# Convolution of tiles 8 to 15 from split operands on unpadded blocks, with moved neighbour parts

## The chip, the cores and the metric

The kernel runs on one core of a Trainium2 chip. Its engines are TensorE (PE; its weight loads are listed as PEld), VectorE (DVE), ScalarE (ACT), GpSimd (POOL) and SyncE (SP), which here only issues DMAs. The engines run side by side and wait for each other by semaphores. The time is that of the device for one launch, in microseconds.

## The reference

Two layers work on x of shape (32, 64, 1024). In a layer a convolution over the last axis (layer 0) or a mixture of eight 1x1 kernels, one set of weights for each sample (layer 1), is followed by a feed-forward product of size 1024 x 1024 with a low-rank part that is chosen for each row by a gate; x is added.

```python
# layer 0
out = lax.conv_general_dilated(x, weight, window_strides=(1,), padding=[(4, 4)],
          dimension_numbers=('NCH', 'OIH', 'NCH'), feature_group_count=4)    # 64 channels, 9 taps, 4 groups
h = out + ctx[:, :, None] + bias[None, :, None]
y = einsum('bsd,od->bso', h, W) + b
sel = the one of x@A[:r].T@B[:, :r].T, r in (8, 16, 32, 64), with the highest score, times its weight
x = x + y + sel
# layer 1: the same shape of work, with einsum('boi,bih->boh', agg_w, x) + agg_b in front,
# and sparsemax weights over 8 experts of rank 16 behind
```

## The kernel before

**Tiles and pairs.** The 32 samples are taken two at a time: a tile is 128 rows (2 samples x 64 channels) of 1024 values; there are 16 tiles. Two tiles are a pair; pairs 0 to 7 are layer 0, pairs 8 to 15 are layer 1. Pairs 0 and 1 are computed plainly while weights are prepared; from pair 2 on (`FULL`) each pair's 256 x 1024 x 1024 product is made from seven products of half size (P1 to P7, Strassen and Winograd's form) of blocks A11, A12, A21, A22 of the mixed input and of their sums S1 to S4 with blocks of the weight and their sums, plus a plain part (`plain`) for the columns that are left.

**Split operands.** The matmuls of the products take a faster form of float32 (fp32r) with fewer bits. So each operand is split: ScalarE casts it to its high part, VectorE subtracts that from the value for the low part (`split_a`, `split_s`, `prep_split`), and TensorE adds three products: high x high, high x low, low x high (`product`, L1379, L1381, L1382).

**The convolution.** The data of a tile is loaded as `blk`: on the partitions 16 channels of a group x 8 positions, in the free dimension 2 samples x 4 groups x 129 blocks of positions (one more than 128, since the rows are padded by 4 on each side). `conv_half(T, n, bank)` (L1328) does one sample: 4 groups x 2 sides, each an unsplit float32 matmul with a block of `blk` stationary and 128 columns of a banded matrix of the taps moving; the second side takes the blocks one further on and adds. VectorE adds the context row and writes the sum to `mixed` (`sum_mix`, L904). TensorE computes the convolution of pair g+1 during pair g, four halves laid between the products, in layer 1 `mix_half` in their place.

**The order of a pair.** It is written out by hand, engine by engine, and each engine follows its list in order. TensorE: plain parts of both tiles, P1, a half, P2, a half, the transpose of the gated rank values (`turn_pair`), P4, P5, a half, the first tile's rank part (`lora`), P6, a half, the second tile's, P7, P3, the rank parts of the second halves. VectorE: gate of the first tile, low parts of S2 and S4, gate of the second, then the sums of the products (`take`), of the plain part (`take_plain`) and of the convolution as they come, the low parts of the next pair's A blocks (L912), of the prepared weights of layer 1 (L861, pairs 3 to 6) and of S1 and S3 (L919). ScalarE: the casts and the gate's exponentials. GpSimd: in pairs 3 to 6 four sums of weight blocks (`prep`, from L529), then the four S sums of the next pair (`sums`, L514 to L522), written in place into `mixed`, after VectorE has made the low parts of the A blocks. SP: loads and stores, in a fixed order.

PSUM has eight banks: b_p0 and b_p1 for the plain parts, b_x, b_y, b_z, b_w for products, b_m and now and then another for the convolution, b_u for transposes.

## Time and profile before

| | us |
|---|---|
| median of 3 runs | 501.63 (501.43 to 501.89) |
| profiled execution | 501.08 |
| its span | 499.3 |
| TensorE busy | 494.9 (99%) |
| VectorE busy | 357.1 (72%) |
| ScalarE busy | 132.5 (27%) |
| GpSimd busy | 141.9 (28%) |

The span runs from the first to the last instruction of the profile; the execution's own time has 1.8 us more around it. Matmuls are pipelined, so that the time that one costs in a stream is read from the start of one to the start of the next (0.20 us for 432 columns), not from its duration (0.36). A line such as L1328 is a line of the kernel; "idle before" says how long the engine stood still ahead of an instruction and what ended that.

### The profile page before, as it was taken

To read this page: it belongs to the slowest core of one execution; us is meant where nothing else is said; L and a number is where in the kernel's file an instruction comes from. 1 tells how busy PE (TensorE), PEld (TensorE's weight loads), DVE (VectorE), ACT (ScalarE), POOL (GpSimd) and SP (SyncE) were. 2 spreads that over 40 slices of the span, in tenths; PEclk is the share of its full clock that TensorE was granted. 3 is DMA by queue.
4 is the path that set the end of the run, shared out by engine and by line. 5 is a ranking of instruction groups with operands and counts; after the bars stand their busy time and mean duration, and the time that the engine had idled before them with its cause. 6 is when DMAs were issued, how large, how long until landed. Compare 5 with 4: busy or idle time off the path is not lost.

```text
span 499.3 us, 8273 instructions
## 1 busy us (share of the span) xinstructions
PE 494.9 (99%) x2921; PEld 459.6 (92%) x2921; DVE 357.1 (72%) x829; ACT 132.5 (27%) x272; POOL 141.9 (28%) x122
## 2 busy tenths in 40 slices
PE   8999999999999999999999999999999999999997
PEld 8989999999999999999999988898998989899886
DVE  4966998758676787767899878676747558675754
ACT  4732344322333123331252321121212112111200
POOL 1000010013444133432205453340616225062520
PEclk9999999999999999999999999999999999999999
DMA  8945205438466475656999553333415232340312
GB/s 319 324 140 175 89 1 159 149 103 267 157 216 220 175 234 189 213 178 224 358 414 347 240 174 101 127 113 130 139 59 173 84 128 105 111 164 1 127 43 84
DMA packets 41124, 84.32 MB, mean 169 GB/s; under 512 B 3803, under 2 KB 16731, under 8 KB 41084
## 3 DMA queue, kind: packets, MB, share of 16 engines
q1 hardware_dynamic: 32028, 61.42, 36.7%
q10 hardware_dynamic: 9056, 22.38, 11.9%
q8 instruction: 23, 0.38, 0.3%
q14 instruction: 17, 0.14, 0.1%
HBM read 58.82 MB, written 24.97 MB: 168 GB/s over the span
## 4 chain that ended last, share of the span: by engine, by line
PE 94%; DMA 2%; DVE 1%; issue 1%; SPq 0%; POOL 0%; ACT 0%; DVEq 0%
PE b_p L1362 9%; PE b_x L1382 7%; PE b_x L1381 7%; PE b_x L1379 7%; PE b_m L1328 5%; PE b_p L1363 4%; PE b_y L1382 4%; PE b_y L1379 4%; PE b_y L1381 4%; PE b_m L1338 3%; PE b_y L1328 3%; PE b_z L1381 2%; PE b_z L1382 2%; PE b_z L1379 2%; PE b_w L1382 2%; PE b_w L1379 2%
## 5 line engine op out<-in xcount | busy, mean ns | idle before, releaser
L596 ACT CAST a_hi<-mixed 128x512 fp32r<-128x512 f32 x63 | 38.1, 620 | 157.5 <-DVE mixed L907 78.6
L1362 PE MATMUL b_p<-wp,a_hi 128*128 128x464 f32 (+1 forms) x224 | 72.6, 377 | 0.0
L542 POOL TENSOR_TENSOR xs<-xs,mixw_sb 128x512 f32<-128x512 f32 x28 | 35.9, 1293 | 121.8 <-DMA xs<-x_scratch 76.0
L919 DVE TENSOR_TENSOR s_lo<-mixed,s_hi 128x512 fp32r<-128x512 f32 x56 | 44.0, 815 | 27.0 <-ACT s_hi L608 27.0
L1363 PE MATMUL b_p<-wp,a_lo 128*128 128x232 f32 (+1 forms) x224 | 60.1, 268 | 0.0
L608 ACT CAST s_hi<-mixed 128x512 fp32r<-128x512 f32 x56 | 34.7, 620 | 86.2 <-POOL mixed L514 50.0
L912 DVE TENSOR_TENSOR a_lo<-mixed,a_hi 128x512 fp32r<-128x512 f32 x63 | 44.3, 731 | 8.8 <-ACT a_hi L596 8.3
L514 POOL TENSOR_TENSOR mixed<-mixed 128x512 f32<-128x512 f32 x13 | 16.7, 1288 | 108.9 <-DVE a_lo L912 108.9
L1362 PEld LDWEIGHTS b_p<-wp,a_hi 128*128 128x128 f32 x224 | 42.1, 188 | 5.1
L1363 PEld LDWEIGHTS b_p<-wp,a_lo 128*128 128x128 f32 x224 | 42.8, 191 | 0.7
L1379 PE MATMUL b_y<-wb_hi,s_hi 128*128 128x464 f32 (+2 forms) x112 | 41.4, 370 | 0.0
L1382 PE MATMUL b_y<-wb_hi,s_lo 128*128 128x464 f32 (+2 forms) x112 | 40.8, 364 | 0.0
L1381 PE MATMUL b_y<-wb_lo,s_hi 128*128 128x464 f32 (+2 forms) x112 | 40.7, 364 | 0.0
L1025 DVE TENSOR_TENSOR xs<-b_x,xs 128x464 f32<-128x464 f32 (+2 forms) x52 | 33.2, 638 | 7.8 <-PE b_x L1382 6.8
L1328 PE MATMUL b_m<-first_in,blk 128*128 128x128 f32 x240 | 29.3, 275 | 0.4 <-DMA blk<-in_xblk 0.4
L1328 PEld LDWEIGHTS b_m<-first_in,blk 128*128 128x128 f32 x240 | 28.9, 192 | 0.7 <-issue 0.5
L1379 PE MATMUL b_x<-wb_hi,s_hi 128*128 128x432 f32 (+1 forms) x80 | 29.3, 367 | 0.0
L1381 PE MATMUL b_x<-wb_lo,s_hi 128*128 128x432 f32 (+1 forms) x80 | 29.2, 365 | 0.0
L1382 PE MATMUL b_x<-wb_hi,s_lo 128*128 128x432 f32 (+1 forms) x80 | 29.1, 364 | 0.0
L1025 DVE TENSOR_TENSOR xs<-b_y,xs 128x512 f32<-128x512 f32 (+2 forms) x26 | 17.0, 654 | 15.8 <-PE b_y L1382 14.2
L1379 PEld LDWEIGHTS b_y<-wb_hi,s_hi 128*128 128x128 f32 x112 | 21.0, 188 | 2.2
L1382 PEld LDWEIGHTS b_y<-wb_hi,s_lo 128*128 128x128 f32 x112 | 21.0, 188 | 1.8
(272 smaller groups left out, 1207.8 us busy)
## 6 DMA issues: line engine op xcount, KB each, us to landing
blk<-x_scratch SPq DMA_DIRECT2D x16, 512.0 KB, 3.9
xs<-in_x SPq DMA_DIRECT2D x30, 256.0 KB, 3.3
x_scratch<-xs SPq DMA_DIRECT2D x30, 256.0 KB, 4.6
blk<-in_xblk SPq DMA_DIRECT2D x14, 516.0 KB, 4.4
xs<-x_scratch SPq DMA_DIRECT2D x28, 256.0 KB, 3.0
out_dram<-xs SPq DMA_DIRECT2D x27, 256.0 KB, 2.1
w_raw<-in_wcat SPq DMA_DIRECT2D x8, 546.0 KB, 8.8
praw<-in_wcat ACTq DMA_DIRECT2D x8, 464.0 KB, 6.1
```

The source lines that it names most:

```text
L542: pool.tensor_tensor(x_rows, x_rows, bbase[:, a:b], ALU.add).then_inc(x_biased[q], 1)
L596: act.copy(a_hi[:, op, :, :], mixed[:, op, :, :]).then_inc(ahi_done[op], 1)
L608: act.copy(s_hi[:, i, :, :], mixed[:, S_AT[i], :, :]).then_inc(shi_done[i], 1)
L912: dve.tensor_tensor(a_lo[:, op, :, :], mixed[:, op, :, :], hi(a_hi[:, op, :, :]), ALU.subtract).then_inc(alo_done[op], 1)
L919: dve.tensor_tensor(s_lo[:, i, :, :], mixed[:, S_AT[i], :, :], hi(s_hi[:, i, :, :]), ALU.subtract).then_inc(slo_done[i], 1)
L1025: dve.tensor_tensor(x_rows, src[:, 0:n], x_rows, ALU.add).then_inc(done, 1)
L1328: ins = pe.matmul(dst, source[:, at + side:at + side + QB], taps, start=(side == 0), stop=(side == 1))
L1362: pe.matmul(both, x_hi, wp[:, k, :, 0:PLAIN[l]], start=(k == 0), stop=False, skip_group_check=True)
L1363: ins = pe.matmul(dst, x_lo, wp_hi[:, k, 0:PLAIN[l]], start=False, stop=(k == NCH - 1), skip_group_check=True)
L1379: pe.matmul(dst, x_hi[:, k, :], w_hi[:, k, :], start=(first and k == 0), stop=False, skip_group_check=not first)
L1381: pe.matmul(dst, x_hi[:, k, :], w_lo[:, k, :], start=False, stop=False, skip_group_check=not first)
L1382: ins = pe.matmul(dst, x_lo[:, k, :], w_hi[:, k, :], start=False, stop=(k == HK - 1), skip_group_check=not first)
```

## The change

For tiles 8 to 15, which are computed during pairs 3 to 6, the convolution takes another form:

- The block is loaded without padding (`xwhole`, 1024 columns). ScalarE casts each sample of it (`cast_x`) and VectorE makes the low part (`low_x`); the taps are split once, at the end of pair 2 (`cast_taps`, `low_taps`).
- A step (`shift_step`) does two groups of one sample: each group three fp32r matmuls with 256 moving columns, for the block of positions itself and, in the same pass, what it gives to its left and right neighbour. Eight steps a pair take the place of four halves.
- VectorE adds the context to the middle 256 columns of the bank (`sum_shift`); ScalarE copies the outer 256 (the neighbours' parts) to SBUF (`take_z`), four DMAs move them by one partition (`move_z`), and GpSimd adds them to `mixed` (`add_z`). The A blocks of those tiles are cast only after that.
- GpSimd's S sums go to a place of their own (`s_sums`) and wait for the products that used them before and no longer for the low parts of A.
- The gates of the two tiles of pairs 2 to 7 are computed together (`gate_scores`, `gate_weights`: the operations of one gate with two tiles side by side, except for two scans and two exponentials).
- In pairs 3 to 6 all engines have a written order of their own (`shift_pair`). In TensorE's P6 now stands ahead of P5. The load of `b_base` moves from pair 3 to pair 7, as its place in SBUF is also used by the cast of x.

The diff, cut to its core; the order of ScalarE and VectorE is shown as rows behind it.

```diff
+def shifted(T):
+    return SHIFTED <= T < TILES
+def steps(T):
+    return 2 * T + 2 * max(0, min(T, TILES) - SHIFTED)
...
+                if shifted(T):
+                    sp.dma_start(blk[T % 2][:, 0:D], xwhole[T - SHIFTED]).then_inc(blk_loaded[T % 2], 16)
...
+            def move_z(T, n):
+                src, dst = z_out[n], z_moved[n]
+                sp.wait_ge(z_taken, 2 * sample(T, n) + 2)
+                if sample(T, n) == 0:
+                    sp.wait_ge(zeroed, 3)
+                if sample(T, n) > 1:
+                    sp.wait_ge(z_added, sample(T, n) - 1)
+                sp.dma_start(dst[1:EDGE + 1, 0, :], src[0:EDGE, 1, :]).then_inc(z_landed[n], 16)
+                sp.dma_start(dst[0:EDGE, 1, :], src[1:EDGE + 1, 0, :]).then_inc(z_landed[n], 16)
+                sp.dma_start(dst[EDGE + 1:P, 0, :], src[EDGE:P - 1, 1, :]).then_inc(z_landed[n], 16)
+                sp.dma_start(dst[EDGE:P - 1, 1, :], src[EDGE + 1:P, 0, :]).then_inc(z_landed[n], 16)
...
             def sums(g):
-                n = 4 * (g - FULL)
-                pool.wait_ge(alo_done[A21], g + 1)
-                pool.wait_ge(alo_done[A22], g + 1)
-                pool.tensor_tensor(mixed[:, A22, :, :], mixed[:, A21, :, :], mixed[:, A22, :, :], ALU.add).then_inc(s_sum, 1)
-                pool.wait_ge(alo_done[A11], g + 1)
+                n, users = 4 * (g - FULL), made(g - 1)
+                pool.wait_ge(p_done[P5], users)
+                if shifted(2 * g):
+                    pool.wait_ge(z_added, sample(2 * g + 2, 0))
+                else:
+                    pool.wait_ge(sum_done, steps(2 * g + 2))
+                pool.tensor_tensor(s_raw(S1), mixed[:, A21, :, :], mixed[:, A22, :, :], ALU.add).then_inc(s_sum, 1)
+                pool.wait_ge(p_done[P7], users)
+                pool.tensor_tensor(s_raw(S3), mixed[:, A11, :, :], mixed[:, A21, :, :], ALU.subtract).then_inc(s_sum, 1)
+                pool.wait_ge(p_done[P6], users)
                 pool.wait_ge(s_sum, n + 1)
-                pool.tensor_tensor(mixed[:, A21, :, :], mixed[:, A11, :, :], mixed[:, A21, :, :], ALU.subtract).then_inc(s_sum, 1)
-                pool.wait_ge(s_sum, n + 2)
-                pool.tensor_tensor(mixed[:, A11, :, :], mixed[:, A22, :, :], mixed[:, A11, :, :], ALU.subtract).then_inc(s_sum, 1)
-                pool.wait_ge(alo_done[A12], g + 1)
+                pool.tensor_tensor(s_raw(S2), s_raw(S1), mixed[:, A11, :, :], ALU.subtract).then_inc(s_sum, 1)
+                pool.wait_ge(p_done[P3], users)
                 pool.wait_ge(s_sum, n + 3)
-                pool.tensor_tensor(mixed[:, A12, :, :], mixed[:, A12, :, :], mixed[:, A11, :, :], ALU.subtract).then_inc(s_sum, 1)
...
+            def add_z(T, n):
+                s = T % 2
+                dst = mixed[:, 2 * s:2 * s + 2, :, CH * n:CH * n + CH].rearrange("p q a c -> p (q a) c")
+                pool.wait_ge(sum_done, steps(T) + 2 * n + 2)
+                pool.wait_ge(z_landed[n], 64 * (T - SHIFTED + 1))
+                pool.tensor_tensor(dst, dst, z_moved[n][:, :, :].rearrange("p v (a c) -> p (v a) c", c=CH),
+                                   ALU.add).then_inc(z_added, 1)
...
+            def cast_x(T, n):
+                act.wait_ge(blk_loaded[T % 2], 16 * (T // 2) + 16)
+                if T == SHIFTED:
+                    act.wait_ge(agg_mm, 3)
+                else:
+                    act.wait_ge(mix_done, steps(T - 1) + 2 * n + 2)
+                act.copy(xh[:, n, :], blk[T % 2][:, BANK * n:BANK * (n + 1)]).then_inc(shift_hi, 1)
+            def take_z(T, n, gp):
+                act.wait_ge(sum_done, steps(T) + 2 * n + gp + 1)
+                if sample(T, n) > 1:
+                    act.wait_ge(z_landed[n], 64 * (T - SHIFTED))
+                src = shift_bank(gp)[:, :].rearrange("p (b a c) -> p b a c", b=4, a=4)[:, 0:4:3, :, :]
+                dst = z_out[n].rearrange("p v (a c) -> p v a c", c=CH)[:, :, :, CH // 2 * gp:CH // 2 * (gp + 1)]
+                act.copy(dst, src).then_inc(z_taken, 1)
...
+            def shift_pair(g):
+                a, b = 2 * g + 2, 2 * g + 3
+                split_s(S2, g)
+                split_s(S4, g)
+                prep_load(g)
+                take_z(a, 0, 0)
+                take_z(a, 0, 1)
+                cast_x(b, 0)
+                gate_exp(2 * g)
+                gate_exp(2 * g + 1)
+                take_z(a, 1, 0)
+                take_z(a, 1, 1)
...
+            def sum_shift(T, n, gp):
+                s, g = T % 2, T // 2
+                dve.wait_ge(s_sum, 4 * (g - 1 - FULL) + (4, 2)[s])
+                for i in (2 * s, 2 * s + 1):
+                    dve.wait_ge(alo_done[i], g)
+                dve.wait_ge(ctx_loaded, 16 * g)
+                dve.wait_ge(mix_done, steps(T) + 2 * n + gp + 1)
+                at = CH * n + CH // 2 * gp
+                row = ctx_row[:, s:s + 1, at:at + CH // 2].to_broadcast([P, POS, CH // 2])
+                dst = mixed[:, 2 * s:2 * s + 2, :, at:at + CH // 2].rearrange("p q a c -> p (q a) c")
+                src = shift_bank(gp)[:, P:P + BANK // 2].rearrange("p (a c) -> p a c", c=CH // 2)
+                dve.tensor_tensor(dst, src, row, ALU.add).then_inc(sum_done, 1)
...
+            def low_x(T, n):
+                part = slice(BANK * n, BANK * (n + 1))
+                dve.wait_ge(shift_hi, 2 + sample(T, n) + 1)
+                dve.tensor_tensor(blk_lo[T % 2][:, part], blk[T % 2][:, part], hi(xh[:, n, :]),
+                                  ALU.subtract).then_inc(shift_lo, 1)
...
+            def gate_scores(g):
+                    dve.tensor_reduce(hid_sb[:, HID0 * s:HID0 * (s + 1)],
+                                      wide(s)[:, :, REST[0]:PLAIN[0]].rearrange("p v c -> p c v"), AX_X,
+                                      ALU.add).then_inc(hid_done, 1)
+                dve.wait_ge(hid_done, 2 * (g - FULL) + 2)
+                hid = by_tile(hid_sb[:, 0:2 * HID0])
...
+            def gate_weights(g):
+                dve.wait_ge(exp_done, 2 * g + 2)
+                link(dve.reciprocal(st[:, 4:6], st[:, 2:4]))
+                link(dve.reciprocal(st[:, 6:8], st[:, 4:6]))
+                link(dve.tensor_tensor(st[:, 0:2], st[:, 4:6], st[:, 6:8], ALU.mult))
+                link(dve.tensor_tensor(kept, below, st[:, 0:2].unsqueeze(2).to_broadcast([P, 2, 4]), ALU.mult))
...
+            def shift_step(T, n, gp):
+                pe.wait_ge(shift_lo, 2 + sample(T, n) + 1)
+                for gl in range(2):
+                    at = QB * (2 * gp + gl)
+                    x_hi, x_lo = xh[:, n, at:at + QB], blk_lo[T % 2][:, BANK * n + at:BANK * n + at + QB]
+                    dst = shift_bank(gp)[:, :].rearrange("p (a c) -> p a c", c=2 * GC)[:, :, GC * gl:GC * (gl + 1)]
+                    w_hi, w_lo = (part[:, gp, 2 * P * gl:2 * P * (gl + 1)].rearrange("p (a c) -> p a c", c=GC)
+                                  for part in (taps_hi, taps_lo))
+                    pe.matmul(dst, x_hi, w_hi, start=True, stop=False)
+                    pe.matmul(dst, x_hi, w_lo, start=False, stop=False)
+                    ins = pe.matmul(dst, x_lo, w_hi, start=False, stop=True)
+                ins.then_inc(mix_done, 1)
+            def emptied(T, n, gp):
+                pe.wait_ge(z_taken, 2 * sample(T, n) + gp + 1)
             def mix_half(T, b, dst_bank):
...
+            def shift_pair(g):
+                t1, t2, a, b = 2 * g, 2 * g + 1, 2 * g + 2, 2 * g + 3
+                if g == AGG_PAIR + 1:
+                    pe.wait_ge(agg_read, 4)
+                pe.wait_ge(sum_done, steps(t2 + 1))
+                if shifted(t2):
+                    emptied(t2, 1, 1)
+                shift_step(a, 0, 0)
+                pe.wait_ge(fin12, g)
+                shift_step(a, 0, 1)
+                pe.wait_ge(fin22, g)
+                product_a(g, P1, b_x, A11, B11)
+                emptied(a, 0, 0)
+                shift_step(a, 1, 0)
+                emptied(a, 0, 1)
+                shift_step(a, 1, 1)
+                pe.wait_ge(fin11, g)
+                product_a(g, P2, b_z, A12, B21)
+                emptied(a, 1, 0)
+                shift_step(b, 0, 0)
+                emptied(a, 1, 1)
+                shift_step(b, 0, 1)
+                turn_pair(g)
+                pe.wait_ge(took_w, made(g - 1))
+                product_a(g, P4, b_w, A22, T4)
+                emptied(b, 0, 0)
+                shift_step(b, 1, 0)
+                emptied(b, 0, 1)
+                shift_step(b, 1, 1)
+                lora(t1, b_z, 0, BANK, c11_done)
+                pe.wait_ge(took_p1, made(g))
+                product_s(g, P6, b_x, S2, T2, first=False)
+                emptied(b, 1, 1)
+                product_s(g, P5, b_y, S1, T1)
+                lora(t2, b_w, 0, BANK, c21_done)
+                pe.wait_ge(took_u2, made(g))
+                product_s(g, P7, b_x, S3, T3, first=False)
+                pe.wait_ge(took_p5, made(g))
+                product_s(g, P3, b_y, S4, B22, first=False)
+                pe.wait_ge(fin21, g + 1)
+                lora(t2, b_x, BANK, D, c22_done)
+                lora(t1, b_y, BANK, D, c12_done)
```

VectorE in pair 4 before, from the second tile's last gate product to the low parts of the prepared weights (`mixed<-b_m,ctx_row` is the convolution's sum, 128x8x64 being 512 columns; `ut_hi` is the transposed rank part; `xs0<-b_x` the sum of P1):

```order
L977 TENSOR_SCALAR u_sb<-hid_sb,kw 128x16
L977 TENSOR_SCALAR u_sb<-hid_sb,kw 128x32
L1025 TENSOR_TENSOR xs0<-b_x,xs0 128x432
L904 TENSOR_TENSOR mixed<-b_m,ctx_row 128x8x64
L904 TENSOR_TENSOR mixed<-b_y,ctx_row 128x8x64
L912 TENSOR_TENSOR a_lo<-mixed,a_hi 128x512 x2
L929 TENSOR_TENSOR ut_hi<-b_u,ut_hi 64x128 x2
L861 TENSOR_TENSOR prep_lo<-praw,prep_hi 128x464 x4
```

VectorE in a pair after, from the same place to P6's sum:

```order
L1257 TENSOR_TENSOR u_sb<-hid_sb,kw 128x2x32
L1135 TENSOR_TENSOR blk_lo<-blk,xh 128x512
L1301 TENSOR_TENSOR xs<-b_x,xs 128x432
L1122 TENSOR_TENSOR mixed<-b_m,ctx_row 128x8x32
L1122 TENSOR_TENSOR mixed<-b_y,ctx_row 128x8x32
L1158 TENSOR_TENSOR ut_hi<-b_u,ut_hi 64x128 x2
L1135 TENSOR_TENSOR blk_lo<-blk,xh 128x512
L1122 TENSOR_TENSOR mixed<-b_m,ctx_row 128x8x32
L1122 TENSOR_TENSOR mixed<-b_y,ctx_row 128x8x32
L1060 TENSOR_TENSOR prep_lo<-praw,prep_hi 128x464 x4
L1301 TENSOR_TENSOR xs<-b_x,xs 128x432
L1140 TENSOR_TENSOR a_lo<-mixed,a_hi 128x512 x2
```

The sums are twice as many and half as wide, two low parts of blocks (`blk_lo`) stand between them, the low parts of A have moved behind P6's sum, and that sum, which P7 waits for, stands behind the low parts of the prepared weights; before, P5's sum did.

ScalarE in a pair after, from the z copies of the second tile's first sample (`a_hi_place<-b_m`, in the space of a_hi's A21) to those of its second:

```order
L849 COPY a_hi_place<-b_m 128x8x32
L849 COPY a_hi_place<-b_y 128x8x32
L777 CAST prep_hi<-praw 128x464 x2
L742 CAST ut_hi<-b_u 64x128
L743 CAST ut_lo<-b_u 64x128
L742 CAST ut_hi<-b_u 64x128
L743 CAST ut_lo<-b_u 64x128
L840 CAST xh<-blk 128x512
L849 COPY a_lo_place<-b_m 128x8x32
L849 COPY a_lo_place<-b_y 128x8x32
```

Before, the casts of A11 and A12 stood around the prep casts in that place; now the block's cast and the z copies do.

GpSimd in a pair after, `mixed<-mixed,z_moved` being the addition of the neighbours' parts, which is new:

```order
L632 TENSOR_TENSOR praw<-praw 128x464
L633 TENSOR_TENSOR praw<-praw 128x464
L635 TENSOR_TENSOR praw<-praw 128x464
L637 TENSOR_TENSOR praw<-praw 128x464
L645 TENSOR_TENSOR mixed<-mixed,z_moved 128x8x64 x4
L617 TENSOR_TENSOR s_sums<-mixed 128x512
L619 TENSOR_TENSOR s_sums<-mixed 128x512
L622 TENSOR_TENSOR s_sums<-s_sums,mixed 128x512
L625 TENSOR_TENSOR s_sums<-mixed,s_sums 128x512
```

Four instructions of 512 columns are put between the prep sums and the S sums, which keep their order.

## Rows read from the trace of the kernel before

**Rows 1.** The page's busy times: us, share of the span, instructions.
```profile
PE 494.9 (99%) x2921; PEld 459.6 (92%) x2921; DVE 357.1 (72%) x829; ACT 132.5 (27%) x272; POOL 141.9 (28%) x122
```
**Rows 2.** TensorE's longest wait: for whom, us in total, times, longest.
```profile
PE b_y L1431 <- POOL ones L489: 1.1, 1, 1.1
```
**Rows 3.** Pairs 4 and 7: length; PE, PEld, DVE, ACT, POOL; clock, DMA share, GB/s.
```profile
144.30:175.04 30.74, 30.74 (x190) 29.36 (x189) 22.72 (x57) 8.31 (x20) 10.92 (x9) 1.00 0.56 186
...
236.50:267.00 30.50, 30.50 (x179) 28.88 (x178) 27.25 (x64) 11.88 (x23) 6.86 (x6) 1.00 1.00 379
```
**Rows 4.** Timeline of TensorE, pair 5: start, duration, line, what.
```profile
182.50 1.95 PE L1328 MATMUL b_m<-first_in,blk 128*128 128x128 f32 x16
184.20 0.44 PE L1379 MATMUL b_z<-wb_hi,a_hi 128*128 128x432 f32 x1
184.48 0.36 PE L1381 MATMUL b_z<-wb_lo,a_hi 128*128 128x432 f32 x1
184.68 0.35 PE L1382 MATMUL b_z<-wb_hi,a_lo 128*128 128x432 f32 x1
```
**Rows 5.** Timeline of TensorE, the last product's twelve matmuls, and the next.
```profile
492.44 0.28 PE L1379 MATMUL b_y<-wb_hi,s_hi 128*128 128x256 f32 x1
...
493.85 0.39 PE L1420 MATMUL b_y<-lb,ut_hi 128*128 128x512 f32 x1
```
**Rows 6.** Timeline of VectorE, pair 4: the second gate (first and last row), sums.
```profile
151.58 0.30 DVE L947 TENSOR_REDUCE hid_sb<-b_p 128x68 f32<-128x136 f32 x1
...
154.40 0.60 DVE L1025 TENSOR_TENSOR xs<-b_x,xs 128x432 f32<-128x432 f32 x1
154.92 0.68 DVE L904 TENSOR_TENSOR mixed<-b_m,ctx_row 128x512 f32<-128x512 f32 x1
...
166.83 0.68 DVE L904 TENSOR_TENSOR mixed<-b_m,ctx_row 128x512 f32<-128x512 f32 x1
167.43 0.60 DVE L1025 TENSOR_TENSOR xs<-b_x,xs 128x432 f32<-128x432 f32 x1
```
**Rows 7.** Timelines of VectorE and of GpSimd, pair 7.
```profile
257.38 2.15 DVE L865 TENSOR_TENSOR wb_lo<-wb_raw,wb_hi 128x928 fp32r<-128x928 f32 x2
...
264.61 3.25 DVE L865 TENSOR_TENSOR wb_lo<-wb_raw,wb_hi 128x928 fp32r<-128x928 f32 x2
...
264.87 2.01 POOL L517 TENSOR_TENSOR mixed<-mixed 128x512 f32<-128x512 f32 x1
266.96 2.05 POOL L519 TENSOR_TENSOR mixed<-mixed 128x512 f32<-128x512 f32 x1
```
**Rows 8.** Timelines of VectorE and of GpSimd, around the end of pair 4.
```profile
174.53 1.29 DVE L919 TENSOR_TENSOR s_lo<-mixed,s_hi 128x512 fp32r<-128x512 f32 x1 [1.60 <-ACT s_hi L608]
175.74 0.68 DVE L1025 TENSOR_TENSOR xs<-b_x,xs 128x512 f32<-128x512 f32 x1
...
173.99 1.29 POOL L517 TENSOR_TENSOR mixed<-mixed 128x512 f32<-128x512 f32 x1
175.35 1.62 POOL L519 TENSOR_TENSOR mixed<-mixed 128x512 f32<-128x512 f32 x1
```
**Rows 9.** Groups of ScalarE: shapes, count, busy us, mean ns, idle before.
```profile
L608 ACT CAST s_hi<-mixed 128x512 fp32r<-128x512 f32 x56 | 34.7, 620 | 86.2 <-POOL mixed L514 50.0 <-POOL mixed L519 14.5 <-POOL mixed L517 11.3
L664 ACT COPY kernels_sb<-b_m 64x512 f32<-64x512 f32 x4 | 2.3, 577 | 0.1
```
**Rows 10.** Pair 4: SP's stores and the loads behind them.
```profile
148.81 0.91 SPq L363 DMA_DIRECT2D x_scratch<-xs  x2
156.45 0.81 SPq L358 DMA_DIRECT2D xs<-in_x  x2
```
**Rows 11.** DMA issues: count, KB each, median us to landing.
```profile
x_scratch<-xs SPq DMA_DIRECT2D x30, 256.0 KB, 4.6
...
praw<-in_wcat ACTq DMA_DIRECT2D x8, 464.0 KB, 6.1
...
aggb_scratch<-aggb_sb SPq DMA_DIRECT2D x1, 8.0 KB, 1.3
```

392 lines of the change are left out of this document (310 added, 82 removed).

## The prediction

> **What bounds the kernel now.** First the busy table and the list of waits: TensorE is busy 494.9 us, 99% of the span [rows 1], and its longest wait, for a constant at the start, is 1.1 us [rows 2]. Then a table of stretches, cut at the starts of layer 0's pairs. I count pairs from 0, and those with converted convolutions are 3 to 6, since pair g convolves for pair g+1. Pair 4 takes 30.74 us and TensorE is busy in all of it, at the full granted clock, with VectorE busy 22.7 us and GpSimd 10.9 us [rows 3]; cut in the same way, pairs 3, 5 and 6 are 30.70, 30.74 and 30.72 us long. So a microsecond taken from TensorE there is a microsecond of the kernel, as long as VectorE, ScalarE, GpSimd and the transfers keep ahead. That cover is what I price.
>
> **TensorE's own work.** A convolution half is sixteen recorded matmuls from 182.50 to 184.20, 1.70 us. The first product behind it takes 0.28 us to the next one instead of 0.20, 0.08 more [rows 4]. Four halves a pair: 4 x 1.78 = 7.12 us. The new form has eight steps a pair, each of 2 groups x 3 matmuls of 256 columns. Such matmuls stand in the last product: twelve from 492.44 to 493.85, 0.118 us each [rows 5]. A step is 6 x 0.118 = 0.71 us, eight are 5.6 us. The transpose, which stood behind a convolution half, now stands between split products; I charge the 0.08 us again. Gain: 7.12 - 5.64 - 0.08 = 1.4 us a pair, 5.6 us in four pairs. The profiled execution took 501.08 us, so without any new wait it would take 495.5.
>
> The Trainium skill (TensorE: Matmul & The Clock Gate, Back-to-back issue gap) gives N/2.4 + 2.5 ns for a warm matmul, 109 ns for 256 columns. The row has 118 ns, so I keep the row. By the page the gain would be 0.4 us a pair larger.
>
> **VectorE's work.** Sums: eight of 256 columns for four of 512. A 512-column one takes 0.60 us to its successor, a 432-column one 0.52 [rows 6]; from that 0.34 for 256, so 2.7 against 2.4 us. Low parts of the blocks: four of 512 x 0.60 = 2.4 us. The gates: one takes 2.82 us (151.58 to 154.40) [rows 6], two 5.6; a joint one has two reduces, one more scan and one set of links, which I put at 1.55 for the scores and 1.4 for the weights, 3.0. Net 0.3 + 2.4 - 2.6 = 0.1 us. By the sum of its work VectorE would have 22.8 of 29.3 us to do, and all would be covered.
>
> **The shared reads.** But look at 264.61: two instructions of VectorE that each read two operands in SBUF take 3.25 us where the same two took 2.15 at 257.38, with GpSimd idle, and in that time GpSimd's two last 2.01 and 2.05 us [rows 7] instead of 1.29 [rows 8]. They run strictly in turn: VectorE waits for GpSimd's end, GpSimd for VectorE's. Instructions that read PSUM are not held: a product's sum at 175.74 keeps its 0.68 us beside a GpSimd instruction. The s_lo ahead of it, held until GpSimd's end at 175.28, takes 1.29 us [rows 8]. In a pair of before GpSimd has 8 such instructions, VectorE 12 large ones. After: 12 (four added z parts) and 16 (four low parts). In turn they fill 12 x 1.26 + 16 x 0.60 = 24.7 us of a pair. What counts is which fall together, so I follow one pair, us from its start, with these durations, 0.22 us from the end of a matmul group to VectorE, and ScalarE's 0.62 for 512 columns and an estimated 0.35 for a z copy of 256 from PSUM, below the 0.58 of one with 512 [rows 9].
>
> TensorE without waits, a product being twelve matmuls of 0.196: plain parts to 5.1; steps of the first new tile a to 5.8 and 6.5; P1 to 8.9; steps to 10.3; P2 to 12.7; steps of tile b to 14.1; transpose and P4 to 16.6; steps to 18.0; rank part; P6 from 18.5 to 20.9; P5 to 23.2; rank part; P7 23.7 to 26.1; P3 to 28.4; rank parts to 29.4.
>
> VectorE comes in late from the pair before (s_lo of S1 and S3 now follow the last sums): it starts S2's and S4's at about 5.9, ends at 7.1; sums of a, 7.8; ScalarE's z copy and cast, then the low part, 9.5; scores 11.0; sums 11.7; weights 13.1 (the transpose wants them at 14.1: covered, by 1 us); low part 13.7; P1's sum 14.2; sums of b 14.9. Here it waits: its rank split stands behind ScalarE's prep casts, these behind GpSimd's prep sums, which wait for the gates; GpSimd starts at 13.7, its second ends at 16.0, ScalarE is through at 17.1 and 17.6, VectorE at 18.0. Low part 19.1 (held by a prep sum, 0.3); sums of b 19.8. GpSimd adds the first z from 19.1 to 20.4, then the second: four prep_lo take until 24.0 instead of 22.1. P6's sum 24.5: **P7 starts at 24.6 instead of 23.7**. a_lo held by the third z, to 26.4; two sums 27.6: **P3 waits for P5's, to 27.7 instead of 27.0**. Plain part, P4's sum 28.9; low part 29.5 to 30.8, as GpSimd is then at the last z or S1's sum or not; P7's sum 30.0 to 31.3, for which the last rank parts wait. The pair ends at 31.1 to 32.4; VectorE goes into the next some 5.9 us late, so this repeats.
>
> The ends: 29.4 a pair if no held read and no wait reaches TensorE; 32.4 if every late term falls together. I take 31.4 for pairs 4 and 5, the lower part of my chain, since a held read can also fall where VectorE would wait anyway. Pair 3 starts less late (four tap and block low parts are added ahead of it, but S4's sum comes 2 us earlier since the sums no longer wait for a_lo): 30.9. Pair 6 has no low parts for a next pair: 30.7. Sum 124.4 us against 122.9 before: +1.5.
>
> **The transfers.** Each moved z is four issues at 0.45 us (two took 0.91 [rows 10]) and lands between 1.3 us (8 KB) and 4.6 us (256 KB) later [rows 11]; 16 issues a pair stand in SP's queue. What queues behind them: the x loads, which wait for stores anyway (issued at 148.81, next loads at 156.45 [rows 10]), and the block loads. A block that lands near 18 instead of 15 holds ScalarE's cast and with it sums of b, but VectorE meets the held prep_lo afterwards in any case; 0 to +0.5 a pair, I take 0. The b_base load moves from pair 3 to pair 7, where the transfer engines are full (1.00 busy against 0.56 [rows 3]); GpSimd needs it only in pair 8: 0 to +1.5 us in all, taken 0. Pair 7 itself has VectorE busy 27.25 of 30.5 [rows 3]; it starts later but its gates are 2.6 us shorter: between 0 and +1.5, taken 0. A gain from layer 1 or these is excluded, since TensorE is full there already. The prep transfer, issued at about 5, takes a median of 6.1 us [rows 11] and is there before the gates. The zeroing of two z buffers and the s_sums that are apart from mixed lie beside TensorE's full time: nothing.
>
> Own time: 501.08 + 1.5 = 502.6 us. The median of the runs shown is 0.55 above the profiled execution; the forecast of the median is **503.1 us**.
>
> **The rivals.**
> A. The cover holds. GpSimd's and VectorE's reads meet less than I lay out, or the joint gate is quicker, so that P7 and P3 start on time; pairs of 29.4 to 30.2 us, 117.6 to 120.8 in all: 496.3 to 499.5. For it: on paper VectorE has 6 us a pair to spare, and 1.3 us less of held reads brings my chain to 29.9. Against it: 24.7 us of reads in turn in 29.4. With the 0.4 us a pair of the page's rule the low end would be 494.7.
> B. The waits just eat the gain: pairs of 30.4 to 31.0, 500.6 to 502.6, within 0.2% of before, which is about what a measurement of this kernel can tell from no change. It is my chain with one held read less in each pair.
> C. Slower by the z chain, one mechanism: the last z part of a pair (TensorE at 18.0, VectorE 19.8, ScalarE 20.2, SP from there behind a 512 KB block load, landing 26 to 27) delays GpSimd's last add, all four S sums and the casts of A21, A22 by that much. Its place is the second plain part, which needs a_lo of A21 2.6 us into the next pair, and A22 at 3.8. In my chain A21 is ready at +2.3 and A22 at +4.1 of a pair of 31.4 in the late variant. So it decides as soon as the landing is later than about 27; each us beyond is a us of the pair. Price 1 to 2 us a pair on top: 505.5 to 509.
> D. That the change doesn't do what it says (six matmuls of 0.118 us a step): output written in runs of 16 floats could slow them; the old form wrote such runs too. 3%.
>
> **Chances.** Forecast (pairs around 31.3, 501.5 to 505.5) 0.40; A 0.33; B beside it 0.11; C 0.13; D 0.03. Faster: A and a little of B and of the forecast's low end, 0.37. Within 0.2%: most of B and the low end of the forecast, 0.17. Slower: the rest, 0.46. For eight in ten the range takes in nearly all of A and the lower half of C: 496.3 to 507.0; the likeliest's own range is 500.8 to 505.5.
>
> **What would show it.** A step of six matmuls in 0.71 us, no more 0.08 behind it. VectorE busy over 26 us a pair, s_lo, a_lo, prep_lo and blk_lo with means well above 0.68 us, GpSimd's instructions above 1.3. TensorE's waits naming P6's and P5's sums on VectorE (took_u2, took_p5), some 1 and 0.7 us a pair. Wrong, if the pairs last 29.4 to 30 us with no such waits (A), if TensorE waits for a_lo at the plain part (C), or if it waits for z copies in ScalarE or for the transpose instead, which I have covered by 1 us only.

## The result and the profile after

| | before | after |
|---|---|---|
| median, us | 501.78 (501.43 to 503.69) | 518.49 (517.11 to 521.45) |
| ratio | | 1.034, 95% interval 1.032 to 1.036 |
| profiled execution | 501.08 | 518.63 |
| its span | 499.3 | 516.8 |

The forecast was 503.1 us, the range 496.3 to 507.0: the sign of the likeliest case was right, the size was not. The page's first line, and from its fourth part the shares of the chain that ended last; they answer to [rows 1]:

```profile
PE 497.5 (96%) x2857; PEld 456.8 (88%) x2857; DVE 364.4 (71%) x797; ACT 152.4 (29%) x322; POOL 167.9 (32%) x140
...
PE 62%; DVE 9%; POOL 9%; DMA 7%; issue 7%; SPq 5%; ACT 1%; DVEq 0%; POOLq 0%
```

TensorE makes up 62% of that chain; VectorE, GpSimd, transfers and SP's issues are in it. What TensorE waited for (us in total, times, longest), answering to [rows 2]:

```profile
PE b_p L1725 <- DVE a_lo L1140: 8.4, 4, 2.4
PE b_y L1742 <- ACT a_lo_place L849: 2.0, 3, 1.1
PE b_y L1742 <- DVE xs L1301: 1.9, 4, 0.6
PE b_z L1701 <- DVE xs L1301: 1.7, 1, 1.7
```

The longest is the second plain part's wait for the low part of A21, once each in pairs 4 to 7. The stretches cut at the starts of pairs 3 to 7 and 0.6 us behind the end of pair 7, columns as in [rows 3], and in the last row 4.3 us behind pair 4's wait:

```profile
114.14:144.37 30.23, 29.74 (x175) 27.66 (x174) 23.69 (x55) 11.63 (x31) 9.94 (x8) 1.00 0.75 238
144.37:178.97 34.60, 31.53 (x175) 29.04 (x174) 25.20 (x53) 13.11 (x32) 17.48 (x12) 0.95 0.61 206
178.97:213.98 35.01, 31.57 (x174) 29.15 (x173) 26.00 (x53) 13.15 (x32) 17.54 (x12) 0.95 0.64 208
213.98:248.46 34.48, 30.58 (x174) 27.61 (x173) 24.73 (x51) 11.91 (x30) 16.70 (x12) 1.00 0.63 200
248.46:281.50 33.04, 28.95 (x162) 26.18 (x161) 25.20 (x51) 14.24 (x26) 11.33 (x8) 1.00 0.97 351
149.20:153.50 4.30, 4.30 (x18) 3.92 (x19) 4.26 (x5) 1.24 (x2) 4.16 (x3) 0.60 0.57 206
```

Pair 3 takes 30.23 us, less than its 30.74 before; pairs 4, 5 and 6 take 34.6, 35.0 and 34.5 against 30.74 each, 11.9 us more. From pair 7's start to the end it is 268.3 us against 262.8, 5.5 more, nearly all of it in pair 7: 32.5 us (248.46 to 280.94) against 27.2 (236.52 to 263.68; the stretch of 30.50 us in [rows 3] runs 3.3 us into pair 8). Pair 3 starts 0.6 later and gives 0.5 back. Together that is the 17.5 us of the span. The later start is there before pair 0: TensorE's first split product begins at 11.4 us instead of 10.7, and anywhere from 10.9 to 12.8 in the kernels of the experiments.

TensorE's own gain is there. The timeline of TensorE where pair 3's first steps begin: twelve matmuls from 119.25 to 120.68, 0.71 and 0.73 us a step.

```profile
119.25 0.28 PE L1686 MATMUL b_m<-taps_hi,xh 128*128 128x256 f32 x1
119.95 0.28 PE L1686 MATMUL b_y<-taps_hi,xh 128*128 128x256 f32 x1
120.68 0.35 PE L1742 MATMUL b_x<-wb_hi,a_hi 128*128 128x432 f32 x1
```

**Where pair 3 goes wrong.** SP's issues of the last two z parts of pair 3 and of the block between them, ScalarE's issue of the store of the prepared weights (0.93 MB twice), and GpSimd's last add:

```profile
135.22 0.82 SPq L433 DMA_DIRECT2D z_moved<-a_hi_place  x1
136.09 0.55 SPq L386 DMA_DIRECT2D blk<-in_xwhole  x1
136.75 0.58 SPq L430 DMA_DIRECT2D z_moved<-a_lo_place  x1
137.37 0.60 SPq L431 DMA_DIRECT2D z_moved<-a_lo_place  x1
138.01 0.85 SPq L432 DMA_DIRECT2D z_moved<-a_lo_place  x1
138.90 1.92 SPq L433 DMA_DIRECT2D z_moved<-a_lo_place  x1
...
137.30 0.39 ACTq L785 DMA_DIRECT2D ts_hi_scratch<-prep_hi  x1
137.72 0.59 ACTq L785 DMA_DIRECT2D ts_lo_scratch<-prep_lo  x1
...
145.71 1.29 POOL L645 TENSOR_TENSOR mixed<-mixed,z_moved 128x512 f32<-128x512 f32 x1 [7.07 <-DMA z_moved<-a_lo_place]
```

The moves of 112 rows are out before or with the store, those of 15 rows behind it. The z part has landed at 145.6, 31.4 us into the pair, where the forecast had 26 to 27.

**The loop.** Pair 4 from its casts of A21 and A22 to those of the next pair, ScalarE, VectorE, GpSimd and SP:

```profile
147.03 1.14 ACT L722 CAST a_hi<-mixed 128x512 fp32r<-128x512 f32 x2 [9.72 <-POOL mixed L645]
...
160.64 0.50 DVE L1257 TENSOR_TENSOR u_sb<-hid_sb,kw 128x16 f32<-128x16 f32 x4
...
161.28 1.52 POOL L632 TENSOR_TENSOR praw<-praw 128x464 f32<-128x464 f32 x1 [7.58 <-DVE u_sb L1257]
166.44 2.99 POOL L645 TENSOR_TENSOR mixed<-mixed,z_moved 128x512 f32<-128x512 f32 x2
180.72 1.27 POOL L645 TENSOR_TENSOR mixed<-mixed,z_moved 128x512 f32<-128x512 f32 x1 [6.87 <-DMA z_moved<-a_lo_place]
...
167.80 0.55 SPq L430 DMA_DIRECT2D z_moved<-a_hi_place  x1
174.05 1.67 SPq L433 DMA_DIRECT2D z_moved<-a_lo_place  x1
...
182.03 1.14 ACT L722 CAST a_hi<-mixed 128x512 fp32r<-128x512 f32 x2 [10.03 <-POOL mixed L645]
```

Low parts, sums, the S low parts and the gates until 161.3 (14.3 us), four prep sums to 166.5 (5.2), the first add to 167.8 (1.3), for which SP's move of the third part waits, nine issues to 175.7 (7.9), landing at 180.7 (5.0), the last add (1.3): 35.0 us, about the length of the pair. Each cast of A21 waits for the chain that the one before it started. TensorE is not in this loop; it waits for it.

### The profile page after: what moved, and what is told of

It is laid out like the page before. It is cut to its first block, busy times and chain, and to the rows that moved or that the text cites. A ratio compares the mean times of both kernels' runs of the same rounds, so it can differ in the third digit from the quotient of the medians.

```text
span 516.8 us, 8425 instructions
## 1 busy us (share of the span) xinstructions
PE 497.5 (96%) x2857; PEld 456.8 (88%) x2857; DVE 364.4 (71%) x797; ACT 152.4 (29%) x322; POOL 167.9 (32%) x140
## 3 DMA queue, kind: packets, MB, share of 16 engines
q10 hardware_dynamic: 9056, 22.38, 11.4%
## 4 chain that ended last, share of the span: by engine, by line
PE 62%; DVE 9%; POOL 9%; DMA 7%; issue 7%; SPq 5%; ACT 1%; DVEq 0%; POOLq 0%
PE b_p L1725 5%; DMA z_moved<-a_lo_place 5%; PE b_x L1745 4%; PE b_x L1744 4%; PE b_x L1742 4%; PE b_m L1673 3%; PE b_p L1726 3%; PE b_y L1745 3%; PE b_y L1742 3%; PE b_y L1744 3%; DMA wp_place<-in_wcat 2%; POOL mixed L645 2%; PE b_m L1701 2%; SPq L432 2%; DVE a_lo L1140 2%
## 5 line engine op out<-in xcount | busy, mean ns | idle before, releaser
L1725 PE MATMUL b_p<-wp,a_hi 128*128 128x464 f32 (+1 forms) x224 | 76.5, 391 | 8.6 <-DVE a_lo L1140 8.4
L654 POOL TENSOR_TENSOR xs<-xs,mixw_sb 128x512 f32<-128x512 f32 x28 | 38.6, 1390 | 122.9 <-DMA xs<-x_scratch 87.8
L1140 DVE TENSOR_TENSOR a_lo<-mixed,a_hi 128x512 fp32r<-128x512 f32 x63 | 54.5, 898 | 20.5 <-ACT a_hi L722 20.0
L733 ACT CAST s_hi<-s_sums 128x512 fp32r<-128x512 f32 x56 | 34.7, 621 | 72.5 <-POOL s_sums L617 34.6
L1148 DVE TENSOR_TENSOR s_lo<-s_sums,s_hi 128x512 fp32r<-128x512 f32 x56 | 46.5, 881 | 7.6 <-POOL s_sums L622 7.4
L1726 PEld LDWEIGHTS b_p<-wp,a_lo 128*128 128x128 f32 x224 | 44.4, 198 | 0.6
L645 POOL TENSOR_TENSOR mixed<-mixed,z_moved 128x512 f32<-128x512 f32 x16 | 22.5, 1411 | 38.1 <-DMA z_moved<-a_lo_place 28.7
L617 POOL TENSOR_TENSOR s_sums<-mixed 128x512 f32<-128x512 f32 x13 | 16.6, 1279 | 56.1 <-DVE mixed L1104 35.2
L1301 DVE TENSOR_TENSOR xs<-b_y,xs 128x512 f32<-128x512 f32 (+2 forms) x26 | 17.1, 656 | 15.8 <-PE b_y L1745 14.3
L659 POOL MEMSET kernels_sb<- 128x2048 f32 x1 | 1.8, 1820 | 66.6 <-DVE wb_lo L1034 66.6
L625 POOL TENSOR_TENSOR s_sums<-mixed,s_sums 128x512 f32<-128x512 f32 x13 | 22.6, 1741 | 1.9
```

Source lines behind the costliest of these rows:

```text
L645: pool.tensor_tensor(dst, dst, z_moved[n][:, :, :].rearrange("p v (a c) -> p (v a) c", c=CH), ALU.add).then_inc(z_added, 1)
L654: pool.tensor_tensor(x_rows, x_rows, bbase[:, a:b], ALU.add).then_inc(x_biased[q], 1)
L733: act.copy(s_hi[:, i, :, :], s_raw(i)).then_inc(shi_done[i], 1)
L1140: dve.tensor_tensor(a_lo[:, op, :, :], mixed[:, op, :, :], hi(a_hi[:, op, :, :]), ALU.subtract).then_inc(alo_done[op], 1)
L1148: dve.tensor_tensor(s_lo[:, i, :, :], s_raw(i), hi(s_hi[:, i, :, :]), ALU.subtract).then_inc(slo_done[i], 1)
L1301: dve.tensor_tensor(x_rows, src[:, 0:n], x_rows, ALU.add).then_inc(done, 1)
```

## The experiments

All start from the changed kernel unless another is named. "Before" ran beside each, between 501.35 and 501.86 us. In brackets behind a time stand its ratio to the kernel before and the 95% interval of that ratio.

**Without the moves.** The four DMAs of `move_z` and the two waits for them go (and one wait for `finq` is added ahead of pair 7's loads); GpSimd adds zeros, and the neighbours' parts are missing from the output.

```diff
-                sp.dma_start(dst[1:EDGE + 1, 0, :], src[0:EDGE, 1, :]).then_inc(z_landed[n], 16)
...
-                pool.wait_ge(z_landed[n], 64 * (T - SHIFTED + 1))
```

> Leaves out the moves: no z DMA is issued, GpSimd adds buffers of zeros, so the neighbours' parts are missing from the output. Theory Z (the last z part of a pair lands too late and holds GpSimd's add, the casts of A21 and A22 and so the second plain part): the plain part's waits (8.4 us in pairs 4 to 7) and the slow clock behind two of them (about 3.4 us) go, and with them most of pair 7's extra: 502 to 505 us. Rival V (VectorE and GpSimd are late by themselves, through their reads in turn, as my forecast had it; the landing is only the last to be seen): the plain part still waits over 1.5 us a pair, 512 to 517 us.

512.83 us (1.024, 1.019 to 1.028): the time is in V's range, but its sign, the plain part's wait, isn't there. Another wait stands in its place: P7 waits 1.7 us in pairs 3 to 5 and 1.2 in pair 6 for P6's sum, with the clock low behind the first and the third of these. GpSimd's adds and VectorE's prep low parts in pair 4, and then the window behind pair 3's wait:

```profile
164.94 6.77 POOL L641 TENSOR_TENSOR mixed<-mixed,z_moved 128x512 f32<-128x512 f32 x4
...
166.33 5.88 DVE L1054 TENSOR_TENSOR prep_lo<-praw,prep_hi 128x464 fp32r<-128x464 f32 x4
```

```profile
140.00:144.00 4.00, 4.00 (x12) 3.70 (x13) 3.96 (x8) 1.66 (x3) 0.56 (x1) 0.57 0.92 336
```

Freed from the transfer, four adds run back to back just where VectorE makes four low parts, and these take 5.88 us instead of 2.59 (at 168.99 in the changed kernel). So both theories were partly right: without Z there is V, the forecast's own.

**A later store.** ScalarE issues `prep_store` behind the casts of S1 and S3, and `prep_load` behind the first z copies.

```diff
-                prep_store(g)
                 split_a(A21, g + 1)
                 split_a(A22, g + 1)
                 split_s(S1, g + 1)
                 split_s(S3, g + 1)
+                prep_store(g)
```

> ScalarE issues the store of the prepared weights (1.86 MB) behind the casts of S1 and S3 instead of ahead of those of A21 and A22, and loads the next raw weights behind the first z copies. Theory Z with the transfer as its main part: the last z lands 3 to 5 us earlier, the plain part's waits and the slow clock go, 503 to 508 us. If instead the late issue counts (SP gets to the last z only at 171.4 us, since GpSimd's prep sums hold the z before it): the landing moves by 1 us, 514 to 517 us. Rival V: no change, 518.

521.07 us (1.037, 1.033 to 1.041), slower than all that was expected, but not for V's reason: the waits for A21 are gone. Pair 4's last moves, issued until 174.55, are added from 175.96; in the changed kernel it was 175.72 and 180.72. From the end of the last issue to the add it is 1.4 us against 5.0: the store had made the difference. What ate it is a new wait of TensorE's, in this kernel's list:

```profile
PE b_m L1686 <- ACT a_lo_place L849: 9.3, 3, 3.6
PE b_u L1770 <- issue: 4.1, 1, 4.1
```

`prep_load` waits for the late store in ScalarE's queue, and the second z copies stand behind it.

**The first add ahead of the prep sums.** GpSimd's `add_z(a, 0)` stands before `prep(g)`; ScalarE's `split_ut` before its first two prep casts.

```diff
+                if shifted(2 * g + 2):
+                    add_z(2 * g + 2, 0)
                 if PREP_FIRST <= g <= PREP_LAST:
                     prep(g)
```

> GpSimd adds the first z part ahead of the four prep sums, ScalarE makes the rank split ahead of the prep casts. Theory Z with the late issue as its main part: SP can move the third z 3 us earlier (it waits for the first add), the last one 2 to 3 us earlier, so the plain part's wait falls to under 0.5 us and the clock stays up: 506 to 511 us. With the transfer as main part: the z still lands together with the prep store, 515 to 518. Rival V: 518, or more, as the prep sums end 2 us later.

505.18 us (1.0067, 1.0046 to 1.0089), 13 us less than the changed kernel and a little better than Z said. Pairs 4 and 5, and the waits:

```profile
144.08:174.80 30.72, 29.95 (x174) 27.61 (x173) 24.71 (x54) 13.11 (x33) 17.01 (x13) 1.00 0.74 235
174.80:205.13 30.33, 29.70 (x174) 27.62 (x173) 24.30 (x54) 13.14 (x33) 17.89 (x13) 1.00 0.73 238
```

```profile
PE b_x L1744 <- DVE xs L1303: 2.5, 4, 0.7
PE b_z L1703 <- DVE xs L1303: 2.1, 1, 2.1
```

The loop of 35 us is gone, and what waits now is P7, for P6's sum, as the forecast had it: 0.5 to 0.7 us in the list, 0.8 from one matmul's start to the next (168.90 less 167.88, where 0.23 is usual, in pair 4).

**ScalarE's order alone**, to part the two edits of that kernel:

> The change with ScalarE's new order alone (rank split ahead of the first two prep casts), GpSimd's order left as it was. It parts the two edits of the kernel that took 505 us. If GpSimd's place for the first add is the cause of the gain: 517 to 519 us. If it was ScalarE's order: 505 to 510.

520.76 us (1.039, 1.037 to 1.042): pairs of 35.0, 36.0 and 33.5 us. ScalarE's order gives nothing by itself, so the gain needs GpSimd's place for the first add; whether that place is enough alone was not run.

**The last z ahead of the block load**, in SP's order:

```diff
-                    load_blocks(b + 2)
                     move_z(b, 1)
+                    load_blocks(b + 2)
```

> SP issues the moves of the last z part ahead of the block load of 512 KB. Theory Z: it gains the load's issue (0.6 us) and 512 KB less ahead of it in the queue (about 1.3 us at 400 GB/s): 1 to 2 us a pair in three pairs, and the clock with it in one or both of two: 510 to 515 us. Rival V: no change, 518.

517.29 us (1.030, 1.028 to 1.033), 1.2 less than the 518.49 of the changed kernel, of another comparison, so no more than a hint. Less than Z said: pair 4's last moves went out from 170.8 instead of 171.4, still with the store.

**TensorE kept busy in the wait.** Eighteen matmuls on the constant ahead of the second plain part's first wait, pairs 4 to 7:

```diff
+                    if k == 0 and s == 1 and FULL + 2 <= g < PAIRS:
+                        for _ in range(18):
+                            pe.matmul(both[:, 0, 0:P], ones[:, :], ones[:, :], start=True, stop=True)
```

> The change with 18 matmuls of 128 columns on the constant (about 1.9 us) ahead of the second plain part's wait in pairs 4 to 7, into a bank that the plain part starts anew. If the idle time itself brings the clock down (0.60 granted behind the waits of pairs 4 and 5): it stays at 1.00, 3 to 3.5 us less: 515 us. If the clock follows something else: 518.5, or 519 where the filling overruns the wait.

520.96 us (1.037, 1.034 to 1.040), although the clock stayed up. Its windows over pair 4's start, and over pairs 4 and 5:

```profile
149.00:153.50 4.50, 4.50 (x38) 4.39 (x38) 4.45 (x5) 2.09 (x4) 4.36 (x4) 1.00 0.44 142
145.39:179.60 34.21, 33.58 (x211) 31.82 (x209) 24.05 (x53) 13.15 (x32) 16.96 (x12) 1.00 0.63 202
179.60:215.29 35.69, 33.95 (x210) 31.62 (x209) 24.83 (x53) 13.12 (x32) 16.87 (x12) 1.00 0.64 211
```

With the waits filled the clock stayed up in pairs 4 and 5, where it had been low behind waits of 2.0 and 2.4 us. That idling alone decides it isn't shown: in the kernel with b_base late (below) a wait of 2.2 us in pair 4 left it at 1.00. Either way the 3.5 us that I had charged to the clock were not in the sum: the pairs keep their 34 to 36 us with TensorE at full clock, since the loop sets them.

**One converted pair** (`SHIFTED = 14`; pairs 3 to 5 keep the old convolution):

> Only tiles 14 and 15 take the new form, in pair 6; pairs 3 to 5 keep the old convolution, with the joint gates, the separate S sums and the late load of b_base. If these parts cost nothing by themselves: pairs 3 to 5 as before at 30.7 us, pair 6 30.2, pair 7 with its wait for A21 (1.9) and its other extra (2 to 3): 504.5 to 506.5 us. If they cost 0.5 us a pair (rival): 506.5 to 508.

505.84 us (1.0075, 1.0058 to 1.0092), in the expected range, but by two misses that cancel: pair 6 took 0.9 us less than expected, the wait for A21 1.6 us more. Pairs 3 to 5 take 30.74 us each, so the joint gates and the separate S sums cost nothing. Pair 6, and pair 7's first 31 us, then its wait:

```profile
206.68:235.96 29.28, 29.28 (x174) 27.88 (x173) 22.53 (x53) 10.79 (x29) 11.03 (x8) 1.00 0.68 211
235.96:267.00 31.04, 27.54 (x151) 25.66 (x150) 23.08 (x49) 12.96 (x25) 9.07 (x7) 0.95 0.93 339
```

```profile
PE b_p L1725 <- DVE a_lo L1140: 3.5, 1, 3.5
```

A converted pair without any wait takes 29.28 us: 1.46 less than before. The wait for the last z, 3.5 us, comes after a single such pair; the loop isn't needed for it, but repeats it.

**P6's sum earlier**, behind two of the four prep low parts, on the kernel with the first add early:

> The change with the first add ahead of the prep sums, and besides VectorE takes P6's sum between the second and the third low part of the prepared weights, so that P7 need not wait for all four. If P7's wait of 0.8 us a pair is this queue position: it falls to under 0.2 us, four pairs, 505.2 - 2.5 to 3.3 = 502 to 502.7 us. If VectorE is simply short of time there (reads in turn), the wait moves to P3 or to the low parts of A and 505 us stays.

507.03 us (1.010, 1.008 to 1.013), slower than both. P7's wait is gone; P3 waits instead (0.6, 0.6 and 0.8 us in pairs 3, 4 and 6), P5 once 1.2 us for a z copy and the mixture 2.8.

**b_base loaded last**, on the changed kernel and on the one with the first add early:

```diff
-                if turns:
-                    sp.wait_ge(mix_done, steps(TILES))
-                    sp.dma_start(bbase, b_base.partition_broadcast(P)).then_inc(s_bbase, 16)
...
                 store_x(2, g)
+                if turns:
+                    sp.dma_start(bbase, b_base.partition_broadcast(P)).then_inc(s_bbase, 16)
```

> The change with the load of b_base (512 KB) issued at the end of SP's list for pair 7 instead of at its start. If this load delays the plain weights (ScalarE's cast, VectorE's low part ahead of P2's sum, 1.8 us in which the mixture waits, and 0.6 behind it): 516 to 517 us. If the delay comes from the late second plain part, behind which that load is issued: 518 to 518.5 us.

> The first add ahead of the prep sums and b_base loaded last, nothing else. In that kernel with the early load the plain weights landed 12.3 us after their issue (8.8 before) and the mixture waited 2.1 us, behind it 1.3 us of slow clock. If the b_base load is the cause: 501.5 to 503 us. If it is the other transfers and VectorE's late start: 505.

518.49 us on the first: the mixture's wait of 1.7 us went, the one for A21 in pair 7 grew to 2.8, nothing was gained. On the second 501.49 us (1.0008, 0.9992 to 1.0024): from 1.0067 to 1.0008 of before, 3.0 us. Its profiled execution is a long one, 503.38 us; pairs 4 and 5, with P7's 0.8 us still in each:

```profile
144.52:174.97 30.45, 29.81 (x175) 27.61 (x174) 24.62 (x55) 13.13 (x33) 17.05 (x13) 1.00 0.74 240
174.97:205.53 30.56, 29.93 (x174) 27.61 (x173) 23.86 (x54) 13.09 (x33) 17.08 (x13) 1.00 0.72 233
```

**VectorE's order**, on that kernel: first the sums of P6 and P5 early, then P7's too.

> The first add ahead of the prep sums, VectorE's sum of P6 behind two of the four prep low parts, its sum of P5 behind one low part of A, b_base loaded last. The products' waits (0.8 us a pair for P7, 0.6 for P3 once P6 is early) and the mixture's 2.1 us of pair 7 should all go: from 505.2 less 4 x 0.8 and less 2 to 3.5 (the clock behind it too): 499 to 500.5 us, faster than before. If VectorE is short in the sum, the waits come back at another instruction: 503 to 505.

506.75 us (1.010, 1.008 to 1.013): no product waits, but the last rank part does, 1.7, 1.8 and 1.7 us in pairs 3 to 5, for P7's sum. So P7's sum goes ahead of the first plain sum and of the block's low part:

```diff
+                take(b_x, 2, g, fin21)
                 dve.wait_ge(fin11, g + 1)
                 take_plain(0, g)
                 if shifted(a + 2):
                     low_x(a + 2, 1)
...
-                take(b_x, 2, g, fin21)
```

> As the kernel with the sums of P6 and P5 early and b_base late (506.8 us, where the last rank part waits 1.8 us a pair for P7's sum), but VectorE takes P7's sum ahead of the first plain sum and of the low part of the block. If VectorE only has its work in the wrong order: no product and no rank part waits, pairs of 29.4 to 30 us, 498 to 500.5 us, faster than before. If VectorE is short of time in the second half of a pair (its reads held by GpSimd's): the wait comes back at a fourth place, A21 or the sums of the convolution, 501.5 to 506.

501.31 us (1.0001, 0.998 to 1.002), just between the two. Pairs 5 and 6:

```profile
175.82:206.01 30.19, 29.75 (x175) 27.80 (x173) 26.17 (x54) 13.09 (x33) 16.42 (x13) 1.00 0.73 235
206.01:235.86 29.85, 29.50 (x174) 27.87 (x173) 24.91 (x55) 11.54 (x31) 15.54 (x13) 1.00 0.76 238
```

Pair 4 is longer, 31.8 us, with a wait of 1.0 us for a z copy; pairs 3 to 6 sum to 121.5 us against 123.0. That order took 5 us off, and 501.3 is where it stopped.

**One pair with both repairs:**

> Only tiles 14 and 15 in the new form (pair 6), with the first add ahead of the prep sums and b_base late. Pair 6 took 29.3 us there against 30.7 before, and pair 7 lost it again by a wait of 3.7 us for A21. With the short z chain that wait should go: pairs 3 to 5 30.74, pair 6 29.4, pair 7 as before or up to 0.5 us more: 500.2 to 501.2 us against 501.4 to 501.8 before. If the wait for A21 stays over 1.5 us: 502 to 504.

503.78 us (1.0049, 1.0022 to 1.0077), worse than expected. Pair 6 took 29.98 us, and A21 was waited for no more; a rank part of layer 1 waited 1.5 us for its weights' low part, a wait that stands in three more of the kernels with the late b_base.

**Fewer, larger moves.** Two of 127 rows in place of two of 112 and two of 15 (and the wait for `finq` as above):

```diff
+                sp.dma_start(dst[1:P, 0, :], src[0:P - 1, 1, :]).then_inc(z_landed[n], 16)
+                sp.dma_start(dst[0:P - 1, 1, :], src[1:P, 0, :]).then_inc(z_landed[n], 16)
```

> The change as it is, but each z part is moved by two DMAs of 127 rows instead of two of 112 and two of 15. The issues of the last two z parts stand one after the other in the chain that I take to set the pair's length (casts of A21, gates, prep sums, adds, z moves, casts of A21): 4 issues of 0.83 us fewer, 3.3 us. If that chain is a loop that sets pairs 4 to 6: 3 us less in each, 508 to 511 us. If the transfer alone counts, or 127 rows move slower (fewer engines get them): 516 to 520.

641.68 us (1.279). The rate of all transfers in 40 slices of 150 to 200 us, and SP's second move in the whole kernel (min, median, max ns of an issue):

```profile
GB/s 24 24 261 364 378 374 282 306 25 25 24 25 25 25 24 25 23 34 216 307 29 25 18 146 243 31 7 375 44 157 413 203 16 18 24 31 24 41 299 279
```

```profile
L431 SPq DMA_DIRECT2D z_moved<-a_lo_place x8: 6428/6932/8262, 131.8 to 356.1; - x8
```

In this stretch nothing else is under way (the last two numbers are the share of the 16 transfer engines' time and GB/s):

```profile
144.60:149.50 4.90, 0.00 (x0) 0.00 (x0) 0.00 (x0) 0.00 (x0) 0.00 (x0) 0.63 0.07 24
```

The core transfers some 25 GB/s, about 1/16 of the 413 that it reaches elsewhere, and 0.07 of the engines' time is busy: one of the 16 carries the move. The Trainium skill (DMA: Bandwidth & Descriptors, Why a DMA increments its semaphore by 16 and not by 1) says so: the number of engines is the largest up to 16 that divides the rows, 1 for 127. The trace agrees. The kernel that had this with the first add, the sums of P6 and P5 early and b_base late:

> Everything of the two before: first add early, the sums of P6 and P5 early, b_base late, two DMAs a z part. With the z chain already shorter than TensorE's work, fewer DMAs give nothing more: as the kernel with the sums early, 499 to 500.5 us. If it is still the chain in some pairs: 0.5 to 1 us less; slower if 127 rows move slowly.

642.34 us (1.281).

**Without the 15-row moves:**

> The change with the two moves of 112 rows alone; those of 15 rows are left out, so 15 partitions of each z lack their neighbour's part in the output. The loop theory (casts of A21, gates, prep sums, adds, the issues of the last two z, landing, add, casts of A21 again: 35 us, and TensorE not in it): 3.3 us of issues less in the loop, pairs 4 to 6 about 31.5 us instead of 34.7, 508 to 511 us. If the landing behind the prep store alone decides, the z land with the store however early they are issued: 515 to 518.

501.17 us (0.9997, 0.998 to 1.002): 17 us less, about twice what was expected of the issues in the loop. Whether the issues or the landings of the 15-row moves count for more, this run can't part. Pair 3's last moves and the store, and the last add:

```profile
134.58 0.51 SPq L430 DMA_DIRECT2D z_moved<-a_lo_place  x1
135.14 0.60 SPq L431 DMA_DIRECT2D z_moved<-a_lo_place  x1
...
137.59 0.39 ACTq L783 DMA_DIRECT2D ts_hi_scratch<-prep_hi  x1
...
138.93 1.51 POOL L643 TENSOR_TENSOR mixed<-mixed,z_moved 128x512 f32<-128x512 f32 x1 [1.87 <-DMA z_moved<-a_lo_place]
```

All moves are out 1.8 us before the store and have landed 3.2 us later. The last add starts 25.3 us into the pair instead of 31.6, and pairs 4 and 5 take 30.3 us.

**The store behind the landing**, one wait more in the changed kernel:

```diff
+                act.wait_ge(z_landed[1], 64 * (b - SHIFTED + 1))
                 prep_store(g)
```

> The change with one wait more: ScalarE issues the store of the prepared weights (1.86 MB) only when the last z part has landed; nothing else is moved. In pair 3 of the change SP issued the last two moves of 15 rows at 138.0 and 138.9 us, behind the store's at 137.3 and 137.7, and they landed at 145.6; without the 15-row moves all z issues were out at 135.7, ahead of the store at 137.6, and landed at 138.9. If this order (last moves behind the store) is what starts the loop of 35 us: the z land 3 to 4 us after their issue, pairs of 30.3 to 31.5 us, 502 to 507 us. If it is the lateness of the issues themselves: 514 to 518 us.

511.15 us (1.019, 1.017 to 1.020), between the two. In pairs 3 to 6 the theory of the store holds: 30.39, 32.77, 30.29 and 30.94 us, 124.4 in the sum where the changed kernel has 134.3 and the one before 123.0, and A21 is never waited for. The rest is lost from pair 7 on, 270.8 us against 268.3 in the changed kernel: the mixture waits 3.9 us there and the transpose 1.8.

**The 15-row moves in pieces of 64 bytes**, on the kernel with all repairs of order:

> The kernel with all repairs of order (first add early, sums of P6, P5 and P7 early, b_base late; 501.3 us), and each 15-row move written as 16 pieces of 64 bytes a row, so that more than one transfer engine may take it. If a move of 15 rows is slow because one engine gets it (as 127 rows did, at 25 GB/s): it lands earlier and the waits left (1.0 us for a z copy in pair 4, 0.35 for A21 in three pairs) go: 498.5 to 500.5 us. If the number of descriptors counts (240 of 64 bytes for 15 of 1 KB): issue and landing get longer, 502 to 510.

502.00 us (1.0009, 0.999 to 1.003): no difference, and the run settles neither theory. Its page and that of the kernel with all repairs of order have the same line of packets:

```profile
DMA packets 46182, 88.47 MB, mean 177 GB/s; under 512 B 4795, under 2 KB 21787, under 8 KB 46140
```

32 moves of 240 pieces would be 7680 packets of 64 bytes. The rows went out whole, as before, and by its packets this is the kernel with all repairs of order once more; its pairs 3 to 6 take 120.0 us in this profile, 121.5 in the other. That 15 rows are no case of 127 is in the trace all the same: 32 moves of 127 rows raise their semaphores in 64 steps, 2 a move; the changed kernel's 64 moves, half of 112 rows and half of 15, in 1024, 16 a move. Why an issue of 15 rows takes 0.82 us stays open.

## Why the prediction was wrong

**TensorE's own work: right.** Eight steps at 0.71 us, 1.4 us a pair: one converted pair without waits took 29.28 us, 1.46 less than before. The gates and the S sums cost nothing, and VectorE was busy 22.5 us in that pair, where pair 6 of before had 22.8 (forecast 0.1 more).

**The shared reads: the mechanism right, its size somewhat too large.** With the first add early P7 starts 0.8 us a pair late, behind P6's sum (forecast 0.9); in the changed kernel P3 is 0.7 late in pairs 3 to 5, behind P5's (0.7). But each kernel has one of the two, not both in a pair, as my chain had it. With the first add early pairs took 30.2 to 30.7 us where I had 31.4. My 503.1 us is nearer to a kernel that was not this one: the one with the first add early and b_base late took 501.5.

**The transfers: the step that failed.** My words were "Each moved z is four issues at 0.45 us", landing "between 1.3 us (8 KB) and 4.6 us (256 KB) later", and for the delay that comes of it "I take 0". Between the 503.1 us and the 518.5 lie 15.4: pairs 4 to 6 took 104.1 us where the sum had 93.5, 10.6 more, and the stretch from pair 7 on 5.5 more, where I had "between 0 and +1.5, taken 0", and where pair 7 of before was 27.2 us with VectorE busy for 23.9, not 30.5 and 27.25 (A21 is waited for 1.7 us there too, the mixture waits 1.7); pair 3 took 0.7 less. Three sizes were wrong. An issue of 112 rows takes 0.57 to 0.60 us, one of 15 rows 0.82 to 0.85: 2.8 us a z part for 1.8. The landing was bounded by rows of other transfers [rows 11], which count from the start of an issue; with the store of the prepared weights, of which the working has no word, it took 6.5 us so counted in pair 4 and 6.7 in pair 3 (5.0 and 4.8 from the issue's end). And I followed a single pair: that a cast of A21 that comes late starts the next round late as well, I priced in rival C at 1 to 2 us a pair on top of my chain, where pairs 4 to 6 took 3.5 more than I had. C's mechanism, its place and its point ("later than about 27") were right; 13% was too little for it, the range stopped in its lower half, and even its upper end, 509, was 9.5 us short.

**b_base: taken 0, bound 1.5, measured 3.0** once the z chain no longer hid it: pair 7 took 31.1 us with the early load and 27.9 with the late one, 27.2 before. Pair 7's transfer engines were full in [rows 3], and the load went to the head of its queue.

**What the runs settle.** The first add behind the prep sums, the store ahead of the last moves and the 15-row moves are each needed for the loop: take away any one, and the waits for A21 vanish. Pairs 4 to 6, 104.1 us in the changed kernel, then take 91.3, 94.0 and 89.9; the later issue of the store lost it again to another wait. Not settled is where the gain of 5.6 us goes in the repaired kernels. With all repairs of order pairs 3 to 6 give 1.5 us of it in one profile and 2.9 in the other; from pair 7 on 0.7 and 2.1 us are lost again, and 0.8 and 0.9 lie ahead of pair 3. Such shares are no larger than what two profiles of one kernel differ by. VectorE is then busy or held for 24 to 26 us of 30, and each sum moved forward made another late, which speaks for its time as the bound; no run took work off it. None of these kernels is faster than the one before.

## What to carry to other kernels

A step that only adds "a small transfer" is a chain: what the issuing queue waits for, its issues one by one, the largest transfer that goes out beside it, and the instruction queued behind its arrival; follow it into the next round, since a chain longer than the round sets the period whatever the busy engine does. Before pricing anything else, look at what stands ahead of the new instruction in each in-order queue: one add moved ahead of four sums was worth 13 us here, together with a change of ScalarE's order that gave nothing by itself. Split a transfer by rows so that the row count divides well over the transfer engines, and issue it ahead of the bulk stores.

## What was not expected of the hardware

- 127 rows in one DMA moved at 25 GB/s; 112 rows and 15 rows apart do not show that. Two of the former a z part cost 123 us over the changed kernel.
- An issue of 15 rows takes SP longer (0.82 us) than one of 112 (0.57).
- After waits of 2.0 and 2.4 us in pairs 4 and 5 the granted clock was 0.60 and 0.62 over some 4.4 us, the lower level in most of it; after 2.2 and 1.7 us in pairs 6 and 7 it stayed at 1.00. Without the moves it was 0.57 and 0.61 after 1.7 us in pairs 3 and 5, and 1.00 after the same 1.7 us in pair 4.
- Four instructions of VectorE that read two operands in SBUF took 5.88 us beside four of GpSimd's, 2.59 us in the changed kernel.
